# A third buffer for the first attention's residual rows, and semaphores by group of heads in the second attention

## What is computed

```python
# layer 0: recurrent attention, 16 heads of 8 channels
x_shift = pad(x)[:, :T]                  # the token before
dd = sigmoid(tanh(x_shift @ ddlerp_w.T))
r, k, v, g, w = projections of lerps of x and x_shift by dd
state = state * exp(w_t) + k_t * v_t;  o_t = state . r_t      # over 512 tokens
x = x + ga * ((groupnorm(o) * g) @ out_w.T)
x = x + gb * (shared_swiglu(h) + sum of the 2 best experts)

# layer 1: local and global attention, 16 heads of 8 channels
x = x + pos_emb
local = softmax(q.k / sqrt(8)) . v       # within windows of 64 tokens
glob  = softmax(x.gt / sqrt(8)) . gt     # gt: 64 compressed + 64 memory rows
mix = sigmoid([local, glob] @ gate_w + gate_b)
out = (mix * local + (1 - mix) * glob) @ out_w + out_b
x = x + ga * out;  x = x + gb * experts(h)
```

## Time and profile before

| | us |
|---|---|
| median of 3 runs | 1292.82 (1291.33 to 1296.19) |
| the profiled execution | 1300.29, its span 1298.5 |
| PE busy | 1151.7 (89% of the span) |
| DVE busy | 834.5 (64%) |
| POOL busy | 597.1 (46%) |
| ACT busy | 504.0 (39%) |
| first attention, 0 to 337 | PE 257.4, DVE 245.4, POOL 218.9, DMA 65% |
| second attention, 518 to 992 | PE 453.4, DVE 325.1, ACT 186.6, DMA 13% |
| steps 3 to 6 of the first attention | 37.7, 44.6, 40.4 and 35.0 long |
| step 4 of the second attention | 51.4 long, 761.97 to 813.39; its last `attend_global` runs 793.31 to 794.37 |

### The profile page before, as it was taken

One profiled execution on the slowest core, in us unless ns is written; L12 is line 12 of the kernel. 1 busy time (PEld: TensorE's weight loads), 2 busy tenths in 40 slices (PEclk: granted clock), 3 DMA queues, 4 the chain that ended last, 5 costly groups with the idle time before them and its releaser, 6 DMA issues.

```text
span 1298.5 us, 24171 instructions
## 1 busy us (share of the span) xinstructions
PE 1151.7 (89%) x8163; PEld 774.4 (60%) x8163; DVE 834.5 (64%) x2229; ACT 504.0 (39%) x1147; POOL 597.1 (46%) x701
## 2 busy tenths in 40 slices
PE   6868768887788888899999999999988699999998
PEld 3445436655358886344454454454444599999994
DVE  4778868778434444535659778786776266666664
ACT  3334424443304443033444444434432245454440
POOL 1466867777625555413144454562245133333330
PEclk9889989797979999989999999999988799999999
DMA  4987587563124522101011021110011331111105
GB/s 133 258 207 178 152 255 186 127 169 93 45 67 119 148 82 64 58 27 45 9 50 48 28 59 32 54 38 18 24 40 49 95 103 36 44 38 38 45 20 203
DMA packets 87314, 113.09 MB, mean 87 GB/s; under 512 B 11224, under 2 KB 68888, under 8 KB 84616
## 3 DMA queue, kind: packets, MB, share of 16 engines
q1 hardware_dynamic: 68120, 86.35, 24.6%
q0 software_dynamic: 8640, 17.84, 4.3%
q10 hardware_dynamic: 10432, 7.35, 2.1%
HBM read 81.06 MB, written 32.04 MB: 87 GB/s over the span
## 4 chain that ended last, share of the span: by engine, by line
PE 63%; issue 10%; DVE 9%; DMA 8%; POOL 4%; ACT 4%; SPq 1%; DVEq 1%; ACTq 0%; POOLq 0%; another core or an unknown queue 0%
PE bank L2122 9%; PE bank L2133 8%; PE bank L2235 5%; PE bank L2284 4%; PE bank L2149 3%; PE bank L1885 3%; PE bank L2293 3%; PE bank L2248 3%; DMA region<-vrdram 3%; PE bank L2312 3%; PE bank L2323 2%; PE bank L1973 2%; DMA xres<-rows 1%; PE bank L2308 1%; PE bank L1944 1%
## 5 line engine op out<-in xcount | busy, mean ns | idle before, releaser
L1275 POOL DMA_INDIRECT slots<-pay,slot x128 | 130.4, 1019 | 132.7 <-issue 109.0
L2122 PE MATMUL bank<-rows,wup 128*128 128x128 f32 x1136 | 156.0, 282 | 17.2 <-DVE wup L764 14.0
L1290 POOL DMA_INDIRECT y<-region,xin x78 | 84.2, 1080 | 156.1 <-ACT region L1694 142.1
L2122 PEld LDWEIGHTS bank<-rows,wup 128*128 128x128 f32 x1136 | 142.0, 197 | 21.5 <-issue 10.0
L1794 ACT ACTIVATE w0uv<-bank 128x512 f32<-128x512 f32 x192 | 99.1, 603 | 129.1 <-PE bank L2293 92.6
L2133 PE MATMUL bank<-rows,wse 128*128 128x128 f32 x1136 | 142.1, 278 | 1.7 <-DVE wse L769 1.7
L2133 PEld LDWEIGHTS bank<-rows,wse 128*128 128x128 f32 x1136 | 132.7, 192 | 7.6 <-issue 6.6
L1885 PE MATMUL bank<-consts 128*128 128x512 f32 x240 | 118.9, 633 | 1.9 <-DVE region L1059 1.9
L1037 DVE TENSOR_REDUCE rows<-bank 128x4 f32<-128x512 f32 x128 | 79.5, 684 | 55.3 <-PE bank L2235 55.0
L1290 POOL DMA_INDIRECT y<-hh,region x64 | 68.8, 1075 | 95.4 <-ACT hh L1694 82.2
L757 DVE SCALAR_TENSOR_TENSOR rows<-bank,bcol,rows 128x128 f32<-128x128 f32 x142 | 43.4, 347 | 92.7 <-ACT rows L1683 92.6
(11 more groups left out here) (359 smaller groups left out, 2381.8 us busy)
## 6 DMA issues: line engine op xcount, KB each, us to landing
region<-vrdram SPq DMA_DIRECT2D x16, 1024.0 KB
region<-vrdram SPq DMA_DIRECT2D x32, 512.0 KB
xin<-slots SPq DMA_DIRECT2D x78, 65.0 KB
region<-slots SPq DMA_DIRECT2D x64, 65.0 KB
wgl<-in_wgl SPq DMA_DIRECT2D x8, 512.0 KB
rows<-y SPq DMA_DIRECT2D x8, 512.0 KB, 4.1
wam<-xres SPq DMA_DIRECT2D x9, 256.0 KB, 2.8
xres<-wam SPq DMA_DIRECT2D x9, 256.0 KB, 2.3
```

The lines of the kernel that those rows point to most:

```text
L1275: p.indirect_dma_start(io["slots"], bass.IndirectOffsetOnAxis(ap=slot_of(l, b)[:, k, t:t + 1], axis=0), pay_of(l, b)[:, k, t, :], None).th ...
L1290: p.indirect_dma_start(io["y"], bass.IndirectOffsetOnAxis(ap=xins[par][:, h, k, P + 1:P + 2].bitcast(U32), axis=0), bYs[par][:, h, k, :], ...
L2122: ins = M(bank_up(l, n)[:, tile(j)], wup[:, n % 3, tile(j)], bxT[:, q % 2, tile(k)], start=True, stop=True)
```

## The change

It has two parts. **(1)** `Xs` gets a third buffer, in the tile of `posT` (the position rows of layer 1), whose load moves from the first attention into the first experts, behind the eight loads of `wgl`. `load_second` moves on ACT from early in step i+1 (for b = i) to step i, behind `key_bank`, and waits for the store of batch i-3. The list `loads_later`, of which SP starts two entries a step, is one shorter; so 2 MB of `w12` start one step earlier, and the pad rows too. **(2)** `c_S` and `c_E` become four semaphores each, one for a group; DVE's maxima and ACT's exponentials wait group by group. For units 1 to 3 the second scores of a group are followed at once by the subtraction of its maximum, where before four and four stood together. `score_local` has its loop over groups outside, so a group's four matmuls stand together. `again_local` takes its wait for the local maxima ahead of its first half. All `keep_busy` fills stay. To have semaphores enough, `a_proj` and `c_proj` are joined, `st_x0` and `st_x1` too, and the eight that tell of loads of y are counts of older ones; none of this adds a wait.

```diff
-        Xs = X, rows[:, 5, :].rearrange(...)
+        Xs = X, rows[:, 5, :].rearrange(...), posT[:, :].rearrange("p (t d) -> p t d", t=NT)
...
-                 (posT[:, :], io["posT"]), (convw[:, :, :], io["convw"]), (gtT[:, G:2 * G], io["gmT"]),
+                 (convw[:, :, :], io["convw"]), (gtT[:, G:2 * G], io["gmT"]),
...
-                   [("load_b", wgl[:, e, :, :], io["wgl"][:, e, :, :]) for e in range(E)])
+                   [... for e in range(E)] + [("load_x", posT[:, :], io["posT"])])
...
             def positions(b, p):
                 v.wait_ge(S["c_hT"], b + 1)
+                if b == 0:
+                    v.wait_ge(S["load_x"], 16)
...
             def max_global(b, t):
-                v.wait_ge(S["c_S"], scores_before(b, t + 1))
                 for g in range(NHG):
+                    v.wait_ge(S[f"c_S{g}"], scores_before(b, t + 1))
                     V.tensor_reduce(maxg[...], bank[g]..., op=ALU.max).then_inc(S["c_mx"], 1)
...  # max_local likewise
             def load_second(b):
-                if b >= 2:
-                    a.wait_ge(S["st_x0"], 16 * (b - 1))
+                if b >= 3:
+                    a.wait_ge(S["st_x"], 16 * (b - 2))
                 settled(a)
-                a.dma_start(Xs[b % 2], xsrc[b]).then_inc(S["load_b0"], 16)
+                a.dma_start(Xs[b % len(Xs)], xsrc[b]).then_inc(S["load_b0"], 16)
...  # ACT, step(i) of the first attention
                 if ok(a):
                     reception(a)
-                if ok(b):
-                    load_second(b)
...
                 if ok(a):
                     key_bank(a)
+                if ok(i):
+                    load_second(i)
                 if ok(c):
                     shared(c)
                     store_second(c)
...
             def exps(b, k):
-                a.wait_ge(S["c_E"], b * E_STEPS + (...))
                 if k >= 2:
                     a.wait_ge(S[f"c_pv{k % 2}"], pv_count(b, k - 2))
...
                 for g in range(NHG):
+                    a.wait_ge(S[f"c_E{g}"], b * E_STEPS + (k + 1 if k < HG else HG + 2 * (k - HG + 1)))
                     A.activation(expT[k % 2][:, g, :], bank[g], ACT.Exp, scale=SCALE).then_inc(S["c_exp"], 1)
...  # score_local
-                for t in range(2):
-                    for w in range(2):
-                        for g in range(NHG):
-                            if t == w == 0:
-                                t_.wait_ge(S["c_exp"], b * UNITS + l * NHG + g + 1)
+                for g in range(NHG):
+                    t_.wait_ge(S["c_exp"], b * UNITS + l * NHG + g + 1)
+                    for t in range(2):
+                        for w in range(2):
                             ins = M(bank[g][...], xTs[p][heads(g), toks], xmk[p][heads(g), :, toks], ...)
...
+            def again_less(b, p, r):
+                if r == 1:
+                    keep_busy(1, bank[6])
+                for g in range(NHG):
+                    bank_free(b, r, g)
+                    M(bank[g], gmk[p][heads(g), r, :], xTs[p][heads(g), :], start=True, stop=False)
+                    M(bank[g], pick_g[heads(g), r, :], negmax[heads(g), :], start=False, stop=True).then_inc(S[f"c_E{g}"], 1)
...  # PE, step(i) of the second attention, for r = 1, 2, 3
-                    again_global(i, p, 1)
-                    less_global(i, 1)
+                    again_less(i, p, 1)
```

More of the change, by code:

```diff
@@ L151, in build @@
         rS = late[:, 0, :]
-        Xs = X, rows[:, 5, :].rearrange("p (t d) -> p t d", t=NT)
+        Xs = X, rows[:, 5, :].rearrange("p (t d) -> p t d", t=NT), posT[:, :].rearrange("p (t d) -> p t d", t=NT)
         kSs, decs = (kS, late[:, 2, :]), (dec, late[:, 3, :])
@@ L531, in _ @@
                        ("load_b", brow[4 * E:8 * E, :], io["bgl"].rearrange("e (j n) -> (e j) n", n=P))],
-                   [("load_b", wgl[:, e, :, :], io["wgl"][:, e, :, :]) for e in range(E)])
+                   [("load_b", wgl[:, e, :, :], io["wgl"][:, e, :, :]) for e in range(E)] + [("load_x", posT[:, :], io["posT"])])
             all_scattered(0)
@@ L2276, in bank_free, with again_global, less_global @@
                     t_.wait_ge(S["c_exp"], b * UNITS + (k - 1) * NHG + g + 1)
-            def again_global(b, p, r):
+            def again_global(b, p):
+                for g in range(NHG):
+                    bank_free(b, 0, g)
+                    M(bank[g], gmk[p][heads(g), 0, :], xTs[p][heads(g), :], start=True, stop=False)
+            def less_global(b):
+                if b == 0:
+                    keep_busy(1, bank[6])
+                t_.wait_ge(S["c_neg"], b * NEG_STEPS + 1)
+                for g in range(NHG):
+                    M(bank[g], pick_g[heads(g), 0, :], negmax[heads(g), :], start=False, stop=True).then_inc(S[f"c_E{g}"], 1)
+            def again_less(b, p, r):
                 if r == 1:
@@ L2284, in again_global @@
                     M(bank[g], gmk[p][heads(g), r, :], xTs[p][heads(g), :], start=True, stop=False)
-            def less_global(b, r):
-                if r == 0:
-                    if b == 0:
-                        keep_busy(1, bank[6])
-                    t_.wait_ge(S["c_neg"], b * NEG_STEPS + 1)
-                for g in range(NHG):
-                    M(bank[g], pick_g[heads(g), r, :], negmax[heads(g), :], start=False, stop=True).then_inc(S["c_E"], 1)
+                    M(bank[g], pick_g[heads(g), r, :], negmax[heads(g), :], start=False, stop=True).then_inc(S[f"c_E{g}"], 1)
             def again_local(b, p, l):
+                if l == 0:
+                    t_.wait_ge(S["c_neg"], b * NEG_STEPS + NEG_STEPS)
                 for bias in range(2):
-                    if bias and l == 0:
-                        t_.wait_ge(S["c_neg"], b * NEG_STEPS + NEG_STEPS)
                     for t in range(2):
@@ L2425, in step @@
                     local_values(i, p)
-                    again_global(i, p, 3)
-                    less_global(i, 3)
+                    again_less(i, p, 3)
                 if ok(a):
```

79 lines of the change are left out of this document (37 added, 42 removed).

## The result

| | median of the runs, us | lowest to highest |
|---|---|---|
| before | 1292.07 | 1288.89 to 1296.19 |
| changed | 1258.55 | 1256.53 to 1264.38 |

A forecast was written before the change was run, and what follows sets the result against it. It took waits to bound the first attention (ACT's for the store of x) and the ring of banks, then DVE, the second. Part 1's 14 us plus part 2's 17 make 31, from a median of 1292.82 to 1262; range 1242 to 1284.

The forecast's parts named there:

- step 4 term of 9.4: First attention, step 4: without ACT's stall for the store, DVE starts unit 6 9.4 us earlier; ends 6 to 13.8.
- step 5's 4: First attention, step 5: half of ACT's 7.6 us wait for the store comes back, 4 us.
- The upper end of part 1, 22: First attention: the most the third buffer and moved loads might save, 22 us, against 14 forecast and 6 at least.
- `w12` earlier: 0, other end 2: First attention: 2 MB more beside step 2's stores delays that step's `mrow`; cost taken as 0, at most 2 us.
- rival 4: First attention, steps 3 to 6: x before store and `mrow` makes `mrow` late; only 2 us remain, 1274; chance 0.06.
- The rings: Second attention, step 4: rounds of scores through PE's banks gain 0.84, 0.49 and 1.15 us, sum 2.5; the step gains 2.4.
- Seven of eight steps have this shape: Second attention: step 4's gain of 2.4 us holds in seven of eight steps, 16.8, say 17 us; ends 0 and 30.
- the unnamed release: Second attention, before `global_sums` on ACT: 1.9 us of idle time after its matmuls, ended by something the profile doesn't name.
- 1 (the second attention gives nothing): Second attention: the unnamed release before `global_sums` sets the step and the rings only wait longer; 1279 us, chance 0.14.
- 5: Both attentions: nothing moves, as both stalls covered DMA and DVE that end at the same time; 1291 us, chance 0.04.
- 2: Second attention: the unnamed release moves with the rings and its 1.9 us go too, 30 us; 1249, chance 0.08.
- 3: Second attention: pairs of one group hold the next on PE, 10 us a step slower; 1359 us, chance 0.06.

The follow-up runs named there:

- e1: The kernel before with only the third buffer, the moved loads of posT and w12 and the earlier load of x; ratio 0.9932 to before.
- e7: Changed kernel with x loaded at its old place and the router's last four of eight indirect DMAs moved later; ratio 0.9677 on the second chip, 0.9728 on the third.
- e2: The changed kernel without part 1: two buffers, posT, w12 and x loaded in their old places; ratio 0.9784 to before.
- e5: The changed kernel with its new order on PE but one semaphore for all first scores and one for all second; ratio 0.9979 to before, second chip.

## Why the prediction was right

1262 was forecast, 1258.55 came. The sign, the two places and the first rings were right; two terms were off to opposite sides, part 1 by 5 us too high and part 2 by 11 too low, so that the sum came nearer than its parts: that much is luck.

- **The waits of ACT for the store** went as said, the step 4 term of 9.4 came out as 7.5 (44.6 to 37.1), step 5's 4 as 4.3, step 6 gave 2.2 for 0.5. DVE was late next, as named: it has no idle time left between units 5 and 6 of step 4, and POOL waited 1.4 for `mrow`. The 36.5 us of waits were never all to be had: `scale_heads` started 8.9, 3.5, 1.4 and 0.4 us after PE's last transpose in steps 4 to 7 (179.63 and 188.48 in step 4), 14.2 in all. The upper end of part 1, 22, is not the sum of the ends given for its terms, 13.8 + 14 = 27.8.
- **"`w12` earlier: 0, other end 2"** was the term that failed in part 1: step 3 grew by 4.1. The argument was that POOL reaches `mrow` late enough. It left out that x now stands ahead of store and `mrow` on the same queue, in the same step in which SP's queue has 2 MB more. That was written as rival 4, which priced it at 12 us less what is covered and gave it to steps 3 to 6; it came in one step. On the second chip the step did not grow, so what was left out is a risk and not a fixed cost. The prediction named a longer wait of POOL for `mrow` as a sign of being wrong; it went from 7.6 to 14.6. Part 1 was 14 in the forecast and is 8.8 alone (e1).
- **The rings** in a step with a router were right nearly to the tenth. Forecast for the second scores of rings 1, 2 and 3: 0.84, 1.33 and 2.5 us earlier. In step 3 they came 0.9, 1.3 and 2.6 earlier (12.30 to 11.43, 20.25 to 18.92, 28.38 to 25.75 from the start of the step), `global_sums` 2.2, DVE's local maxima 1.4 where 1.3 was said. At equal clock such a step lost 2.3 (51.4 to 49.1), with 2.4 forecast. That they would be capped by `global_sums` and DVE's full second half held there.
- **"Seven of eight steps have this shape"** was the term that failed in part 2. Steps 0 to 2 have no router on PE between the banks' release and the second scores, DVE has 5 us less to do in them, and no indirect DMAs lie there. What had been put down as covered wasn't: only step 4 was read for the forecast, where DVE had 1.4 and 1.8 us to win before the maxima of the second and third ring, and in step 2 it was 3.9 and 5.3. Ring 1 gained 1.8 and not 0.84, and the steps gave 6.4, 4.3 and 4.3, 15.0 for a forecast of 7.2. (Step 0 goes with the clock too: 56.3 at 0.87 in before, 50.0 at 0.89 in the changed kernel, and in e7 on the second chip 47.8 at 0.94.) Steps 3 to 6 gave 4.2, -0.9, 2.5 and 2.9, 8.7 for 9.6, with the clock moving single steps by 2. The last step, for which nothing was forecast, gave 5.5 up to the fill behind its last `attend_local` (969.98 in before, 929.86 in the changed kernel). Part 2 was 17 in the forecast and is 28.0 alone (e2), near the end of 30, though not by the way that stood for it (the unnamed release, which stayed).
- **How PE treats groups.** The rows contradicted the strict order of matmuls in the Trainium skill, "TensorE: Matmul & The Clock Gate", section "The mechanism"; the result decides for the rows. Held pairs of one group let the next group by: sixteen instructions of four groups in 2.45 us, and no 1.39 between groups. Another page of the Trainium skill, "TensorEngine Tiling (Array Packing)", section "Tiling Modes", has different tiles execute matmuls in parallel; with that the rows here agree.
- **The rivals.** 1 (the second attention gives nothing) and 5 fell with e2; 2 was wrong in its way and near in size; 3 fell; 4 was true for one step. What was said to break the sum, a lower clock, cost some 3.2 us in step 4 (52.3 at 0.93, where step 3 took 49.1 at 1.00), which so came out 0.9 longer than before's.

## What to carry to other kernels

A signal for all of four parts makes whoever waits for it wait for the last, and here the order of the parts then gained nothing; split the signal first, and put the parts in the order of the signals second. Price a step of a pipeline in each of its shapes (with and without the router here): the gain of one was twice that of the other. When a buffer frees a transfer to start earlier, look at what it now stands before on its queue: here the buffer's gain could be kept and the transfer left where it was. When a view names who ended a wait, look at when the others that it could have been ended too, and at the same place in more than one step.

## What the hardware showed that was not expected

- A row of indirect DMAs on POOL, 0.96 us each and 1.26 apart, beside DVE's maxima held back the start of an ACT instruction, which shares nothing with them that the trace shows, by 1.6 to 2.1 us after its matmuls' end. It was so in every kernel with the eight DMAs at that place on two chips, and in none of three on another.
- A version that took 1.6 us of waiting out of each step had no gain from it: its granted clock was 1.00 in one step and 0.93 in the next two, which were 3.6 and 3.9 us longer.
- Chips differ: before took 1260.8, 1294.7 and 1301.2 us on the three. Steps 1 and 2 of the second attention have the same length on all, wherever the same order of work was traced. From the last batch's first unit in the first attention to the start of the second, with the first experts in it, it is 262 us for before on the first and 238 for e5 on the second.
